# LayerNorm, linear attention and a ternary FFN on eight cores: z1 transposed on TensorE, weights quantized on ScalarE, attention matmuls moved ahead of the first FFN matmul

## The reference, cut to what matters

```python
def attn(x, Wqkv, bqkv, Wout, bout):            # x: [8, 4096, 1024]
    q, k, v = split(x @ Wqkv + bqkv, 3)
    q = q / norm(q); k = k / norm(k)
    kv = sum(k * v, axis=tokens)                # one row of 1024 per sequence
    return (q * kv) @ Wout + bout

def ternary_quant(w):
    scale = 1 / clip(mean(|w|), 1e-5)
    return clip(round(w * scale), -1, 1) / scale

def ffn(x, g1, b1l, w1, b1, g2, b2l, w2, b2):   # hidden size 4096
    h = layer_norm(x, g1, b1l) @ ternary_quant(w1).T + b1
    h = layer_norm(gelu(h), g2, b2l)
    return h @ ternary_quant(w2).T + b2

x = x + attn(layer_norm0(x), ...)               # layer norm without gain and bias
x = x + ffn(x, ...)
```

## Time and profile before

| | us |
|---|---|
| median of 3 runs (3268.43 to 3373.88) | 3288.59 |
| the profiled execution | 3254.23 |
| its span on the slowest core (core 4) | 3252.6 |
| of which phase A / between / phase B | 1118 / 142 / 1992 |
| busy: PE / DVE / ACT / POOL | 1615.2 / 1052.2 / 624.8 / 291.2 |

### The profile page before, as it was taken

The page is one execution under the profiler, slowest core; times in us unless marked ns, Lnnn a source line. Parts: engine busy times, 40 slices in busy tenths (PEclk is TensorE's granted clock), DMA queues, the critical chain, the costliest instruction groups (busy, mean ns, idle before and its releaser), DMA issues.

```text
span 3252.6 us, 34550 instructions; the slowest of 8 cores (3232.0 to 3252.6 us)
## 1 busy us (share of the span) xinstructions
PE 1615.2 (50%) x10545; PEld 893.5 (27%) x10672; DVE 1052.2 (32%) x2522; ACT 624.8 (19%) x1185; POOL 291.2 (9%) x265
## 2 busy tenths in 40 slices
PE   1143534331135524474564665665655656656657
PEld 0011211110012211342342433433433423423424
DVE  1464366533334323032132232231231231331332
ACT  0132322210023200211211211211201202202202
POOL 2111012147730000000000000000000000000000
PEclk9977766665578757787787777777777777877878
DMA  9845244424312290100110110010110110110010
GB/s 147 209 152 158 79 141 165 124 81 132 114 68 68 59 177 16 32 31 26 36 32 24 37 33 23 29 40 17 35 41 17 35 42 17 33 43 17 30 30 21
DMA packets 242871, 212.10 MB, mean 65 GB/s; under 512 B 195588, under 2 KB 195589, under 8 KB 242695
## 3 DMA queue, kind: packets, MB, share of 16 engines
q0 software_dynamic: 31200, 92.34, 10.4%
q1 hardware_dynamic: 192768, 75.58, 9.8%
q10 hardware_dynamic: 18728, 41.97, 3.4%
HBM read 117.52 MB, written 58.72 MB: 54 GB/s over the span
## 4 chain that ended last, share of the span: by engine, by line
PE 41%; SPq 15%; DVE 10%; issue 9%; DMA 7%; ACT 6%; DVEq 5%; POOL 3%; POOLq 3%; ACTq 1%; another core or an unknown queue 0%
PE py L663 15%; PE py L687 14%; PE pqkv L567 6%; SPq L315 5%; PE patt L645 5%; SPq L307 4%; DMA wstg<-w 3%; SPq L275 3%; POOLq L489 2%; DVEq L757 2%; POOL qog L482 1%; SPq L296 1%; DVE outbuf L996 1%; DVE xring L917 1%; DMA qT<-qhscr 1%
## 5 line engine op out<-in xcount | busy, mean ns | idle before, releaser
L567 PE MATMUL pqkv<-wqkvp,h1T 128*128 128x512 bf16 x1505 | 388.3, 421 | 686.3 <-DVE qkvb L787 376.3
L663 PE MATMUL py<-w2p,h4buf 128*128 128x512 bf16 x1968 | 532.4, 400 | 110.0 <-DVE outbuf L1004 103.9
L687 PE MATMUL py<-z1T,w1p 128*128 128x256 bf16 x4096 | 481.7, 282 | 122.5 <-ACT h4buf L438 102.5
L954 DVE TENSOR_TENSOR h4sq<-h4buf 128x128 bf16<-128x128 bf16 x1024 | 224.3, 225 | 766.2 <-PE psumQ L672 731.8
L687 PEld LDWEIGHTS py<-z1T,w1p 128*128 128x128 bf16 x4096 | 381.5, 100 | 219.0 <-issue 127.9
L567 PEld LDWEIGHTS pqkv<-wqkvp,h1T 128*128 128x128 bf16 x1536 | 160.8, 106 | 913.4 <-issue 771.3
L645 PE MATMUL patt<-woutp,qT 128*128 128x512 bf16 x496 | 148.3, 465 | 512.4 <-DMA qT<-qhscr 511.5
L438 ACT ACTIVATE h4buf<-py,beta1c 128x256 bf16<-128x256 f32 x512 | 240.5, 473 | 228.6 <-PE py L687 228.0
L645 PEld LDWEIGHTS patt<-woutp,qT 128*128 128x128 bf16 x512 | 57.2, 114 | 600.7 <-issue 568.3
L917 DVE TENSOR_TENSOR xring<-patt,xbufB 128x1024 f32<-128x1024 f32 x32 | 39.2, 1224 | 514.6 <-PE patt L645 510.4
L672 PE MATMUL psumQ<-onesb,h4sq 128*128 128x1 bf16 x1024 | 167.5, 164 | 76.5 <-DVE h4sq L954 76.5
(11 more groups left out here) (118 smaller groups left out, 1237.8 us busy)
## 6 DMA issues: line engine op xcount, KB each, us to landing
wstg<-w POOLq DMA_DIRECT2D x128, 512.0 KB, 6.3
xbufA<-x SPq DMA_DIRECT2D x32, 512.0 KB, 4.3
xbufB<-x SPq DMA_DIRECT2D x32, 512.0 KB, 3.5
out<-outbuf ACTq DMA_DIRECT2D x32, 512.0 KB, 2.6
h1scr<-h1buf ACTq DMA_DIRECT2D x32, 256.0 KB, 4.2
qhscr<-qhat ACTq DMA_DIRECT2D x32, 256.0 KB, 2.0
wq1scr<-qod POOLq DMA_DIRECT2D x32, 256.0 KB, 3.1
z1scr<-z1buf ACTq DMA_DIRECT2D x32, 256.0 KB, 2.0
```

Of the source, the lines that this page charges most:

```text
L567: mm = te.matmul(out=pq[i % 4][:, :], lhsT=h1T[:, (g % 2) * 4096 + c * 512 + s * 128: (g % 2) * 4096 + c * 512 + (s + 1) * 128], rhs=wqkvp ...
L663: mm = te.matmul(out=py2[:, hh * 512:(hh + 1) * 512], lhsT=h4m, rhs=w2p[:, m * D + hh * 512:m * D + (hh + 1) * 512], start=(m == 0), stop= ...
L687: mm = te.matmul(out=py1[m % 2][:, :], lhsT=w1p[:, c * H + m * 128:c * H + (m + 1) * 128], rhs=z1T[:, c * 256:(c + 1) * 256], start=(c == ...
L954: bsq.inc(dv.tensor_tensor(out=h4sq[:, (m % 4) * 128:(m % 4 + 1) * 128], in0=h4m, in1=h4m, op=ALU.mult))
```

## The change

1. **z1 is transposed on PE.** `z1scr`, its write and the transposing DMAs of `z1T` go. PE multiplies each 128x128 block of `z1buf` by an identity matrix into the PSUM tile `pzT`, four blocks at a time (`zT_round`, twice per tile); DVE copies each block to `z1T` (`zT_evac`). `psumS` and `psumQ` become one tile, `psumSQ`.
2. **The order in phase B.** `attn_mm(j0+2)` goes ahead of y1, and `sc_front(j0+2)` ahead of the Gelus.
3. **The quantization.** For each of the 64 chunks ACT computes Sign(w*s - 0.5) and Sign(w*s + 0.5) in bf16, four chunks per iteration from u = 10 on, and DVE adds the two. The sum is twice the ternary value, so gains and layer norm biases are multiplied by 0.5. POOL only issues DMAs. Four result buffers instead of two.
4. **DVE's order in phase A.** `dv_consume` comes after `dvA_back` instead of before it, and DVE waits for `gmld` at its very start, to halve `b1lc` and `b2lc`.

```diff
@@ SP, phase B
-                sy.wait_ge(bz1w.h, 16 * (j + 1))
-                if j >= 4:
-                    sy.wait_ge(by1.h, 32 * (j // 2))
-                for c in range(8):
-                    bz1t.inc(sy.dma_start(
-                        out=z1T[:, c * 256 + (j % 2) * 128:c * 256 + (j % 2) * 128 + 128],
-                        in_=z1_d[j * 128:(j + 1) * 128, c * 128:(c + 1) * 128],
-                        transpose=True), j)
@@ ACT, phase A
+            def sc_consume(n, u):
+                for _ in range(n):
...
+                    if kind == "w1q" and u < min(10, NT - 1):
+                        return
+                    if kind == "w2q" and u < min(18, NT - 1):
+                        return
...
+                    sc.wait_ge(wld.h(i % 5), 16 * (i // 5 + 1))
+                    if kq >= 4:
+                        sc.wait_ge(dvw.h(kq - 4), 16 * ((kq - 4) // 4 + 1))
...
+                    sc.activation(out=abuf, in_=wslot(i), func=AF.Sign,
+                                  scale=scol, bias=mcols[:, 5:6])
+                    scq.inc(sc.activation(out=bbuf, in_=wslot(i), func=AF.Sign,
+                                          scale=scol, bias=mcols[:, 4:5]))
             for j in range(NT):
                 scA_front(j)
                 if j >= 3:
                     scA_back(j - 3)
+                    sc_consume(4, j - 3)
@@ ACT, phase B
                 if t >= 1:
-                    sc.wait_ge(bz1w.h, 16 * t)
+                    sc.wait_ge(bzt.h, 2 * t)
...
             for p in range(NT // 2):
                 j0, j1 = 2 * p, 2 * p + 1
+                if j0 + 2 < NT:
+                    sc_front(j0 + 2)
...
-                if j0 + 2 < NT:
-                    sc_front(j0 + 2)
                 sc_tail(j0)
@@ PE, phase B
+            def zT_round(t, r):
+                g = 2 * t + r
+                if r == 0:
+                    te.wait_ge(bz1.h, t + 1)
+                if g >= 1:
+                    te.wait_ge(bze.h, g)
+                for cc in range(4):
+                    c = 4 * r + cc
+                    mm = te.matmul(out=pzT[:, cc * 128:(cc + 1) * 128],
+                                   lhsT=z1buf[:, c * 128:(c + 1) * 128],
+                                   rhs=identb[:, :], start=True, stop=True)
+                bzt.inc(mm)
@@ DVE, phase A
+            dv.wait_ge(gmld.h, 16 * 5)
+            dv.tensor_scalar(out=b1lc[:, :], in0=b1lc[:, :], scalar1=0.5,
+                             scalar2=None, op0=ALU.mult)
...
+                    dv.wait_ge(scq.h, kq + 1)
+                    dcons.inc(dv.tensor_tensor(out=dst, in0=dst, in1=srcb,
+                                               op=ALU.add))
...
                 dvA_front(j)
-                if NT >= 32:
-                    dv_consume(6)
...
                 if j >= 3:
                     dvA_back(j - 3)
                     dvA_extra(j - 3)
+                if NT >= 32:
+                    dv_consume(6, j)
@@ DVE, phase B
+            def zT_evac(t, r):
+                g = 2 * t + r
+                dv.wait_ge(bzt.h, g + 1)
+                for cc in range(4):
+                    c = 4 * r + cc
+                    cp = dv.tensor_copy(
+                        out=z1T[:, c * 256 + (t % 2) * 128:c * 256 + (t % 2) * 128 + 128],
+                        in_=pzT[:, cc * 128:(cc + 1) * 128])
+                bze.inc(cp)
...
                 if j0 + 2 < NT:
                     dv_front(j0 + 2)
+                    zT_evac(j0 + 2, 0)
+                    zT_evac(j0 + 2, 1)
...
                 dv_h4sq(j1)
+                if j1 + 2 < NT:
+                    zT_evac(j1 + 2, 0)
+                    zT_evac(j1 + 2, 1)
                 dv_tail(j1)
```

More of the change, by code:

```diff
@@ L219, in build_program @@
             cons_engine.append("dv")
-        elif kind == "w1q":
+        else:
             cons_engine.append("dv")
-        else:
-            cons_engine.append("gp" if ch % 2 == 0 else "dv")
     gp_ord = {}
@@ L284, in _ @@
             sy.wait_ge(bar.h, 5)
-            sy.wait_ge(dvw.h(0), 16 * 16)
-            sy.wait_ge(dvw.h(1), 16 * 16)
+            for sl in range(4):
+                sy.wait_ge(dvw.h(sl), 16 * 8)
             for c in range(8):
@@ L327, in _ @@
             smld.inc(sc.dma_start(out=onesrow[:, :], in_=onesrow_d.ap()), 16)
+            smld.inc(sc.dma_start(out=identb[:, :], in_=ident_d.ap()), 16)
             def scA_front(j):
@@ L416, in sc_front @@
                                       bias=stB[:, P + 7:P + 8]))
-                sc.wait_ge(bz1.h, t + 1)
-                bz1w.inc(sc.dma_start(out=z1_d[t * 128:(t + 1) * 128, :],
-                                      in_=z1buf[:, :]), 16)
             def sc_tail(j):
@@ L711, in _, with dv_consume @@
             dvq_pos = [0]
-            def dv_consume(n, limit=None, max_i=None):
+            def dv_consume(n, jcur, limit=None, max_i=None):
                 for _ in range(n):
@@ L719, in dv_consume @@
                         return
-                    kind0 = wplan[dvq_loads[k0]][0]
-                    if kind0 == "w1q" and m1r.n == 0:
-                        return
-                    if kind0 == "w2q" and m2r.n == 0:
+                    i0 = dvq_loads[k0]
+                    kq0 = dvq_of_load.get(i0)
+                    if kq0 is not None and (kq0 >= len(sc_emit_tile)
+                                            or sc_emit_tile[kq0] > jcur - 3):
                         return
@@ L852, in _ @@
                     dvA_extra(j - 3)
+                if NT >= 32:
+                    dv_consume(6, j)
+                else:
+                    dv_consume(64 // NT + 1, j, limit=NW1 + NW2)
             for u in range(max(0, NT - 3), NT):
@@ L855, in _ @@
                 dvA_extra(u)
-            dv_consume(10 ** 9)
+            dv_consume(10 ** 9, NT + 999)
             dv.wait_ge(kvc.h, 8)
```

165 lines of the change are left out of this document (84 added, 81 removed).

## The result

The changed kernel took 2788.96 us (median of 10 executions, 2779.52 to 2981.59), the kernel before 3259.69 in the same rounds: a ratio of 0.8547, 95% interval 0.851 to 0.8583. (Medians here are over all executions; ratios leave out those in which one group of cores was slowed.) The forecast was 2805, with 2705 to 2910 around it. The profiled execution took 2815.5 us, with spans from 2759.8 to 2813.9 by core; the forecast for it was 2776.

The account below looks back on a forecast made before the run. The prediction took both phases to be bound by waits, chiefly PE's for `qT` in phase B and POOL's quantization pace in phase A. 3254.2 - 396 - 82 = 2776 us profiled, 2805 as a median, range 2705 to 2910.

Parts of the forecast that it names:

- Phase B, -396: Attention and MLP pairs: 25.1 us less per pair, 98.2 us each; 396 us less in all, bounds -330 and -430.
- the wait for `qT`: PE's second attention matmul in each pair of phase B: its wait goes, -32.1 us per pair.
- the ring: Behind that wait in phase B: `patt` emptied, z1 written, SP's `z1T` transposes (10.0 us), then `qT`'s, 10 us more.
- the longer chain (+9.5): Start of a pair, up to y1's third block: 18.0 us instead of 8.5, PE standing for 10 to 11.
- The casts: DVE's PSUM copies of transposed z1: four in 0.9 us, bounds 0.8 and 2.8; a round 1.4 us.
- The Sqrt table: First Sqrt after the Gelus, now in `sc_tail(j0)`: its table load makes PE wait, +1.3 us per pair.
- Phase A, -82: Phase A: quantization on ACT gives -85 us, the start costs +3; bounds -125 and -30.
- The start, +3: Start of phase A: DVE waits for `gmld` until 77.8, front 0 at about 90; +3 us, bounds 0 and +14.
- Load chain on POOL: Rival, 14%: phase A's four chunks add 15.3 us per iteration instead of 10, so it gains nothing; median 2890.
- Tables: Rival, 4%: Sign is not in Sqrt's table set, so ACT loads twice per phase A iteration, 41 us; median 2846.
- The clock at half: Rival, 4%: PE granted 1.2 GHz throughout phase B, +55 us per pair, 880 in all; median 3690.
- Part without effect: Rival, 3%: phase B's 32 us return as a wait for casts or `sc_front`; about 3270 with phase A's part lost.

Follow-up runs that it names:

- second part alone: Kernel before with z1 transposed on PE, attn_mm(j0+2) ahead of y1, sc_front ahead of the Gelus, old quantization; ratio 0.8802 to the kernel before.
- first part alone: Kernel before with Signs on ACT, bf16 sum on DVE, reordered DVE iteration and early gmld wait, old attention and transposes; ratio 0.9705 to the kernel before.
- four loads ahead: Changed kernel with POOL writing the quantized block of load i-4 rather than i-2 before issuing load i; ratio 0.8473 to the kernel before.
- combined kernel: Changed kernel with late gmld wait, four loads ahead, dummy Sqrt behind the Gelus and transposing rounds inside y2; ratio 0.82 to the kernel before.

## Why the prediction was right, point by point

**Phase B, -396.** Measured alone: -390, by the profiled executions -387. A pair was to be 98.2 us and is 98.9. Term by term: the wait for `qT` is gone (-32.1); the second attention is warm (3.62); the chain from the rounds to the third block is 17.9 where 18.0 was worked out, PE's idle 10.71 where 10 to 11 was said. Its mechanism was right as well, and the experiments name its shares: with the transposes taken first, 20.4 us of the wait go with the trip of z1 and 11.65 with the order. The prediction had put the whole 32.1 down to the order and nothing to the transposes beyond the ring; the order alone brings none of it (33.0 remain), so the wait goes only by both. What the prediction didn't see is that `sc_front` needn't have moved: it priced the longer chain (+9.5) as the cost of the order, while it is the cost of one of two moves, the one without which the kernel is 3.3 us a pair faster. By the traces (second part alone against before, mean of the cores) the first pair gave -40 where -48 was foreseen, the fourteen pairs -346 where -351 was, and the last -1 where +3 was. The -346 hold a bit of luck: thirteen of the steps are steady ones at -24.1 and not -25.1, and the step to the last pair gave -32, since no attention and no front stands ahead of its y1 any more, which the prediction didn't count.

**The casts.** Four in 0.88 us, 283 ns each, within the 0.9 taken; a round 1.5 us, with 1.14 of waiting, for 1.4.

```profile
1200.44 0.88 DVE L1038 CAST z1T<-pzT 128x128 bf16<-128x128 f32 x4
```

**The Sqrt table.** The load of 1.28 us stands in `sc_tail(j0)` as foreseen, and starts only when DVE's result is there:

```profile
1869.69 1.28 ACT L460 ACT_TABLE_LOAD   x1 [22.44 <-DVE stB L1007]
1870.98 0.20 ACT L460 ACTIVATE stB<-stB 128x1 f32<-128x1 f32 x1
```

The Sqrt follows 0.01 us behind the load. The Trainium skill, "ScalarE: Activation LUTs", section "What ACT_TABLE_LOAD costs", counts a drain of 1380 ns beside the load's 1283; the trace has nothing of it. The term of 1.3 was right for PE's wait (8.0 against 6.7 us, in two kernels that take it away), but taking it away by itself brought 0.5 a pair.

**Phase A, -82.** attn(0) starts 81 us earlier in the mean of the cores (1252.2 to 1171.2), 77 with the first part alone, 96 by the ratio of that run and 92 against the run with the old phase A on its chip; the bounds held all of these. The stretch from front 13 to 31 was to be 548 and is 544 on core 0; in the mean of the cores it lost 85.2 us (626.5 to 541.3), where -85 was foreseen. The sum of two bf16 tiles takes 0.69 us where 0.7 was taken, against 1.28 for the same size with one fp32 operand. The Trainium skill, "VectorE: DVE Perf Modes", section "Mode 2×_1P — pack two bf16 into one 32-bit read", gives two results a cycle for 16-bit operands; the trace agrees, with a little over half the time. ACT's fourth load is late as said:

```profile
587.32 1.24 ACT L410 ACTIVATE qtd<-wstg,mcols 128x1024 bf16<-128x1024 f32 x1 [2.99 <-DMA wstg<-w]
```

It landed 5.3 us after its issue where 4.7 was taken. Yet most iterations were 24 to 27 us against 26.8 (those at a group's start 48 to 50 against 47.4). So this chain was somewhat cheaper than worked out: with four loads ahead, an iteration falls by 1.9 us and not by the 2.99 of ACT's wait.

**The start, +3.** Front 0 at 88 (90 foreseen), front 3 12 us late instead of 7 and front 13 still 5 us late (408.1 against 403.1, means of the cores; core 0 now, 411.13, must not be held against core 4 before, 411.72). With the wait taken out, the fronts 13 and 31 come 9 and 10 us earlier. So at the end of the loop it cost more than the 3, within the bounds of 0 to 14.

**The rivals.** Load chain on POOL: it ends the iterations, but within the 10 us that the sum had for it, and 1.9 of them. Tables: ACT loads none between Sqrt and Sign in phase A. The clock at half: no. But the profiled execution of the changed kernel is 26 us above its median and 39 above the 2776 forecast for it; the last section shows some 34 us on its slowest core that come from the clock. Part without effect: no. That 2805 was above the 2789 measured has a plain reason: the factor 1.0106 from one execution to the median of the first three runs. The ten runs beside the changed kernel had a median of 3259.69, not 3288.6; with the sum of -478 they would give 2782. Measured are -471.

## What to carry to other kernels

A queue that carries two transfers in a fixed order is one ring: before you move the work of one, take the other out, and test each edit alone, since here the new order by itself, both moves together, cost 1.8% and with the transposes off the queue it gained 10 us a pair. When two instructions are moved as one edit, price them apart: the matmuls' move was the whole gain, the statistics' move behind it a loss of 3.3 us a pair, 5.6 in the combined kernel. And a wait taken off PE's path needn't shorten it by as much, as PE's matmuls may take longer in its place. Before a small difference between two profiles is given a cause, look at what kernels with the same code in that stretch show: here attn(0) alone spreads by 14 us among them.
